# Local attention in blocks of 32 queries by 64 keys, with the queries' inverse norms applied inside the softmax

## The reference, cut to what matters

```
q, k, v = split(x @ Wqkv)                        # per layer; n = 1024, two sequences, 16 heads of 64
q = l2norm(q) * qs;  k = l2norm(k) * ksc         # t / max(norm(t), 1e-12)
q = q * cos * scale + rotate_half(q) * sin * scale
k = k * cos * inv   + rotate_half(k) * sin * inv
# windows of w = 32: a window's queries see its own keys and those of the window before
mask = (it < jb) | (it > jb + w) | (jb == -1)
sim  = where(mask, -max, einsum(q, k) * 8)
out  = einsum(softmax(sim), v) @ Wo
```

## Time and profile before

| | |
|---|---|
| median of 3 runs (lowest to highest) | 2109.58 us (2108.05 to 2110.93) |
| the profiled execution, its span | 2105.7 us, 2103.9 us |
| PE, DVE, ACT, POOL busy | 1906.2, 1582.6, 1596.2, 1665.0 us (91%, 75%, 76%, 79%) |
| mean granted TensorE clock | 0.973 of full speed |
| DMA queue of SP | 97.59 MB, 17.8% of 16 engines' span |

### The profile page before, as it was taken

One profiled execution on the slowest core, in us unless ns is written; L12 is line 12 of the kernel. 1 busy time (PEld: TensorE's weight loads), 2 busy tenths in 40 slices (PEclk: granted clock), 3 DMA queues, 4 the chain that ended last, 5 costly groups with the idle time before them and its releaser, 6 DMA issues.

```text
span 2103.9 us, 67397 instructions
## 1 busy us (share of the span) xinstructions
PE 1906.2 (91%) x22192; PEld 1444.0 (69%) x22192; DVE 1582.6 (75%) x4006; ACT 1596.2 (76%) x5607; POOL 1665.0 (79%) x1252
## 2 busy tenths in 40 slices
PE   5992899998999998899989899988999998999986
PEld 3661678774777774777774677774777774777772
DVE  4766788876788876788876788876788876888865
ACT  4871788885888884888874888884888875888872
POOL 2123999985999976899976899976899976999960
PEclk9995999999999999999999999999999999999998
DMA  2001222110321111211111311111211111112110
GB/s 64 14 12 51 79 50 56 45 46 11 99 51 45 45 46 31 83 48 45 45 46 28 84 50 45 45 46 35 81 46 45 45 46 36 47 45 56 49 29 21
DMA packets 44547, 99.43 MB, mean 47 GB/s; under 512 B 7344, under 2 KB 24208, under 8 KB 43504
## 3 DMA queue, kind: packets, MB, share of 16 engines
q1 hardware_dynamic: 44400, 97.59, 17.8%
HBM read 19.59 MB, written 1.05 MB: 10 GB/s over the span
## 4 chain that ended last, share of the span: by engine, by line
PE 70%; issue 12%; POOL 8%; ACT 5%; DVE 4%; POOLq 0%; DVEq 0%; DMA 0%; ACTq 0%; SPq 0%
PE bank L1124 9%; PE bank L1137 8%; PE bank L1151 7%; PE bank L1172 7%; PE bank L1117 7%; PE bank L1153 6%; PE bank L1158 6%; PE bank L1152 6%; PE bank L1108 3%; ACT kT L525 2%; POOL rn L321 2%; POOL ropeL L358 2%; POOL tsum L323 2%; PE bank L1164 2%; PE bank L1255 2%
## 5 line engine op out<-in xcount | busy, mean ns | idle before, releaser
L321 POOL TENSOR_TENSOR rn<-n2c,half_neg 128x8 f32<-128x8 f32 x384 | 636.4, 1657 | 81.8 <-DVE n2c L793 81.0
L487 ACT ACTIVATE prob<-bank,nmax 128x96 f32<-128x96 f32 x1536 | 501.2, 350 | 130.6 <-DVE nmax L743 130.4
L323 POOL TENSOR_TENSOR tsum<-tc_,ts_ 128x512 f32<-128x512 f32 x384 | 489.3, 1274 | 0.0
L326 POOL TENSOR_TENSOR w_nat<-tsum,rn 128x512 f32<-128x512 f32 x384 | 400.6, 1043 | 37.8 <-POOL tsum L323 15.1
L786 DVE TENSOR_REDUCE n<-nat 128x8 f32<-128x512 f32 x384 | 262.3, 683 | 138.2 <-ACT nat L503 126.8
L487 ACT ACTIVATION_READ_ACCUMULATOR prob<-bank,nmax 128x1 f32 x1536 | 331.4, 216 | 0.0
L743 DVE TENSOR_REDUCE nmax<-bank 128x4 f32<-128x384 f32 x384 | 196.1, 552 | 153.7 <-PE bank L1117 146.5
L496 ACT ACTIVATE pT<-bank 96x512 f32<-96x512 f32 x384 | 230.3, 600 | 74.6 <-PE bank L1124 72.4
L1151 PE MATMUL bank<-w_hi,xs 128*128 128x512 f32 x576 | 275.1, 478 | 12.6 <-DVE ts_ L796 9.7
L796 DVE TENSOR_TENSOR ts_<-bank,ropeL 128x256 f32<-128x256 f32 x768 | 285.8, 414 | 0.0
L1124 PE MATMUL bank<-idf,prob 128*96 128x128 f32 x1536 | 245.9, 284 | 42.9 <-ACT kT L525 28.2
(11 more groups left out here) (126 smaller groups left out, 3331.0 us busy)
## 6 DMA issues: line engine op xcount, KB each, us to landing
vspace<-v_nat SPq DMA_DIRECT2D x96, 384.0 KB, 4.0
vspace<-v_nat SPq DMA_DIRECT2D x96, 256.0 KB, 3.4
vspace<-v_nat SPq DMA_DIRECT2D x95, 128.0 KB, 2.3
nat<-w_qkv SPq DMA_DIRECT2D x5, 1536.0 KB, 8.0
wo<-w_o SPq DMA_DIRECT2D x6, 512.0 KB, 4.0
w<-w SPq DMA_DIRECT2D x6, 341.0 KB, 3.1
shared<-w_qkv SPq DMA_DIRECT2D x1, 1536.0 KB, 7.0
w<-w SPq DMA_DIRECT2D x6, 192.0 KB, 3.1
```

Of the source, the lines that this page charges most:

```text
L321: nc.gpsimd.tensor_tensor(rn[:, r, :], n2c[:, r, :], half_neg[:, 0:8], ALU.pow).then_inc(pool_step, 1)
L323: nc.gpsimd.tensor_tensor(tsum[:, r, :], tc_[:, r, :], ts_[:, r, :], ALU.add).then_inc(pool_step, 1)
L326: nc.gpsimd.tensor_tensor(w_nat[:, r, :].rearrange("p (h d) -> p h d", d=D), tsum[:, r, :].rearrange("p (h d) -> p h d", d=D), rn[:, r, :] ...
L487: last = nc.scalar.activation(prob[:, 4 * b + i, :], SB[b][:, i * SPAN:(i + 1) * SPAN], ACT.Exp, bias=nmax[:, p, 8 * G + 4 * b + i:8 * G + ...
```

## The change

The queries of a tile are taken in four blocks w of 32 (`BLOCKS`), each with the 64 keys that it can see (`SEEN`), instead of two halves of 64 with 96 keys. So the banks SB hold 4 x 64 columns rather than 4 x 96, the exponentials are 128x64, and two heads fill the 128 columns of one transpose. `transpose_probs` and `probs_out` run once per group rather than twice, and wait for all eight exponentials. `scores` and `weigh_values` issue 32 matmuls per group (64 instructions in a trace) rather than 16, each with 32 rather than 64 weight columns. The values lie in `vw` in four blocks and twice, by head parity, on partitions 0 to 63 and 64 to 127, moved by ten DMAs rather than three. `weigh_values` writes two banks (half of bank 5, part of bank 7).

The queries' inverse norms stay in `rnq`: POOL no longer multiplies the queries by them (two of four `L326` per tile go, and its loop now takes two tiles). `exps` gets them as a per-partition scale, and `maxima` writes the raw maximum into four spare columns of the score bank and multiplies it by `rnq` in a second instruction. `heads_out` multiplies in two instructions of 256 columns.

The order is rewritten too. On PE both halves of `project_out` stand together behind `transpose_heads(t, 3)`; ring bank 4 takes all transposed heads, bank 6 the probabilities and outputs. On ACT `square(t+1, 3)` stands ahead of `probs_out(t, 1)`. On DVE `residual` is for tile t-1, and stands between `rotary(t+1, 1)` and `maxima(t, 1)`.

```diff
@@ -17,0 +18,2 @@
+BLOCKS, SEEN = P // WIN, 2 * WIN
...
@@ -102 +106,2 @@
-        rn = sb("rn", [P, 2, 8])
+        rn = sb("rn", [P, 8])
+        rnq = sb("rnq", [P, 2, HEADS])
...
@@ -131 +137,3 @@
-        PJ, SB, OB, YB = bank[0:2], bank[2:4], bank[5], bank[7]
+        PJ, SB, YB = bank[0:2], bank[2:4], bank[7]
+        OB, O2 = bank[5], (bank[5][:, 0:HB // 2], bank[7][:, P:P + HB // 2])
...
@@ -247,2 +264,7 @@
-                eng.dma_start(vw[WIN:SPAN, p, 0, :], v_nat[0:HALF, p, :]).then_inc(v_seen[p], 16)
-                eng.dma_start(vw[:, p, 1, :], v_nat[WIN:P, p, :]).then_inc(v_seen[p], 16)
+                for b in range(2):
+                    eng.dma_start(vw[b * SEEN + WIN:(b + 1) * SEEN, p, 0, :].rearrange("p (g c) -> p g c", g=2),
+                                  four_heads(p, b, 0, WIN)).then_inc(v_seen[p], 16)
+                for w in range(1, BLOCKS):
+                    for b in range(2):
+                        eng.dma_start(vw[b * SEEN:(b + 1) * SEEN, p, w, :].rearrange("p (g c) -> p g c", g=2),
+                                      four_heads(p, b, (w - 1) * WIN, SEEN)).then_inc(v_seen[p], 16)
@@ -251 +273,7 @@
-                    eng.dma_start(vw[0:WIN, 1 - p, 0, :], v_nat[P - WIN:P, p, :]).then_inc(v_prev[1 - p], 16)
+                    for b in range(2):
+                        eng.dma_start(vw[b * SEEN:b * SEEN + WIN, 1 - p, 0, :].rearrange("p (g c) -> p g c", g=2),
+                                      four_heads(p, b, P - WIN, WIN)).then_inc(v_prev[1 - p], 16)
+            def four_heads(p, b, row, rows):
+                return v_nat[row:row + rows, p, :].rearrange("p (g b c) -> p g b c", g=2, b=2)[:, :, b, :]
...
@@ -321 +350,8 @@
-                    nc.gpsimd.tensor_tensor(rn[:, r, :], n2c[:, r, :], half_neg[:, 0:8], ALU.pow).then_inc(pool_step, 1)
+                    if r == 0:
+                        at_least(eng, p_ready, t * 4 - 4)
+                        nc.gpsimd.tensor_tensor(rnq[:, p, cols], n2c[:, r, :], half_neg[:, 0:8], ALU.pow).then_inc(pool_step, 1)
+                        eng.wait_ge(pj_dve, Q + 1)
+                        at_least(eng, tp_full, Q - 1)
+                        nc.gpsimd.tensor_tensor(w_nat[:, r, :], tc_[:, r, :], ts_[:, r, :], ALU.add).then_inc(w_ready, 1)
+                        continue
+                    nc.gpsimd.tensor_tensor(rn[:, :], n2c[:, r, :], half_neg[:, 0:8], ALU.pow).then_inc(pool_step, 1)
...
@@ -486 +523,2 @@
-                    head = 8 * G + 2 * i + b
+                    h = 2 * i + b
+                    slot = 2 * (h % 4) + h // 4
@@ -488,2 +526,4 @@
-                        prob[:, 4 * b + i, :], SB[b][:, i * SPAN:(i + 1) * SPAN], ACT.Exp,
-                        bias=nmax[:, p, 8 * G + 4 * b + i:8 * G + 4 * b + i + 1], accum_out=lsum[:, p, head:head + 1])
+                        probs[:, slot * SEEN:(slot + 1) * SEEN], SB[b][:, i * SEEN:(i + 1) * SEEN], ACT.Exp,
+                        scale=rnq[:, p, 8 * G + h:8 * G + h + 1],
+                        bias=nmax[:, p, 8 * G + 4 * b + i:8 * G + 4 * b + i + 1],
+                        accum_out=lsum[:, p, 8 * G + h:8 * G + h + 1])
@@ -492 +532 @@
-            def probs_out(t, G, b, at):
+            def probs_out(t, G, at):
@@ -494,3 +534,3 @@
-                eng.wait_ge(pt_full, t * 4 + (2 * G + b + 1))
-                at_least(eng, pv_done, t * 2 + G)
-                nc.scalar.activation(pT[:, 4 * b:4 * b + 4, :], RING[at][0:SPAN, :].rearrange("p (h q) -> p h q", h=4),
+                eng.wait_ge(pt_full, t * 2 + (G + 1))
+                at_least(eng, pv_done, t * 2 + (G - 1))
+                nc.scalar.activation(pT[:, 4 * G:4 * G + 4, :], RING[at][:, :].rearrange("p (h q) -> p h q", h=4),
...
@@ -599 +638,0 @@
-                    probs_out(t, 0, 0, 6)
@@ -602 +641 @@
-                    probs_out(t, 0, 1, 4)
+                    probs_out(t, 0, 6)
@@ -609,2 +648,3 @@
-                        heads_T(t + 1, 1 - p, 0, 6)
-                    probs_out(t, 1, 0, 4)
+                        heads_T(t + 1, 1 - p, 0, 4)
+                        square(t + 1, 3)
+                    probs_out(t, 1, 4 if closing else 6)
@@ -614 +653,0 @@
-                        square(t + 1, 3)
@@ -616,3 +655,2 @@
-                        heads_T(t + 1, 1 - p, 1, 6)
-                    probs_out(t, 1, 1, 6)
-                    heads_out_T(t, 0, 4)
+                        heads_T(t + 1, 1 - p, 1, 4)
+                    heads_out_T(t, 0, 4 if closing else 6)
...
@@ -743,3 +782,8 @@
-                    nc.vector.tensor_reduce(nmax[:, p, 8 * G + 4 * b:8 * G + 4 * b + 4],
-                                            SB[b][:, 0:4 * SPAN].rearrange("p (h k) -> p h k", h=4),
-                                            AX.X, ALU.max, negate=True).then_inc(max_ready, 1)
+                    nc.vector.tensor_reduce(SB[b][:, 4 * SEEN:4 * SEEN + 4],
+                                            SB[b][:, 0:4 * SEEN].rearrange("p (h k) -> p h k", h=4),
+                                            AX.X, ALU.max, negate=True).then_inc(raw_ready, 1)
+                for b in range(2):
+                    eng.wait_ge(raw_ready, t * 4 + (2 * G + b + 1))
+                    eng.wait_ge(pool_step, t * 6 + (1 + 3 * G))
+                    nc.vector.tensor_tensor(nmax[:, p, 8 * G + 4 * b:8 * G + 4 * b + 4], SB[b][:, 4 * SEEN:4 * SEEN + 4],
+                                            rnq[:, p, 8 * G + b:8 * G + 8:2], ALU.mult).then_inc(max_ready, 1)
@@ -750,2 +794 @@
-                hs = slice(8 * G, 8 * G + 8)
-                nc.vector.reciprocal(linv[:, p, hs], lsum[:, p, hs]).then_inc(linv_ready, 1)
+                nc.vector.reciprocal(linv[:, p, 8 * G:8 * G + 8], lsum[:, p, 8 * G:8 * G + 8]).then_inc(linv_ready, 1)
@@ -753,4 +796,7 @@
-                nc.vector.tensor_tensor(
-                    o_nat[:, G, :].rearrange("p (h d) -> p h d", d=D), OB[:, :].rearrange("p (h d) -> p h d", d=D),
-                    linv[:, p, hs].rearrange("p (h o) -> p h o", o=1).to_broadcast([P, 8, D]),
-                    ALU.mult).then_inc(o_evac, 1)
+                for b in range(2):
+                    h0 = 8 * G + 4 * b
+                    last = nc.vector.tensor_tensor(
+                        o_nat[:, G, b * HB // 2:(b + 1) * HB // 2].rearrange("p (h d) -> p h d", d=D),
+                        O2[b].rearrange("p (h d) -> p h d", d=D),
+                        linv[:, p, h0:h0 + 4].rearrange("p (h o) -> p h o", o=1).to_broadcast([P, 4, D]), ALU.mult)
+                last.then_inc(o_evac, 1)
@@ -918,2 +963,0 @@
-                        if not (isinstance(n, int) and n == 1):
-                            residual(t - 2, n - 2)
@@ -925,0 +970,2 @@
+                    if not opening:
+                        residual(t - 1, n - 1)
...
@@ -1108,2 +1153,2 @@
-                    nc.tensor.matmul(SB[b][:, 0:4 * SPAN], idb[:, :].bitcast(bf16),
-                                     msk[:, n, :].bitcast(bf16).rearrange("p (o k) -> p o k", o=1).to_broadcast([P, 4, SPAN]),
+                    nc.tensor.matmul(SB[b][:, 0:4 * SEEN], idb[:, :].bitcast(bf16),
+                                     mskB[:, n, :].bitcast(bf16).rearrange("p (o k) -> p o k", o=1).to_broadcast([P, 4, SEEN]),
@@ -1112,3 +1157,3 @@
-                    g, cols = 4 * G + i, slice(i * SPAN, (i + 1) * SPAN)
-                    for half in range(2):
-                        qs, ks = slice(half * HALF, (half + 1) * HALF), slice(half * HALF, half * HALF + SPAN)
+                    g, cols = 4 * G + i, slice(i * SEEN, (i + 1) * SEEN)
+                    for w in range(BLOCKS):
+                        qs, ks = slice(w * WIN, (w + 1) * WIN), slice(w * WIN, w * WIN + SEEN)
@@ -1121,2 +1166,3 @@
-            def transpose_probs(t, G, b, at):
-                eng.wait_ge(p_ready, t * 4 + (2 * G + b + 1))
+            def transpose_probs(t, G, at):
+                eng.wait_ge(p_ready, t * 4 + (2 * G + 2))
@@ -1124 +1170,2 @@
-                    last = nc.tensor.transpose(RING[at][0:SPAN, i * P:(i + 1) * P], prob[:, 4 * b + i, :], idf[:, :])
+                    last = nc.tensor.transpose(RING[at][:, i * P:(i + 1) * P], probs[:, 2 * i * SEEN:2 * (i + 1) * SEEN],
+                                               idf[:, :])
...
@@ -1130,2 +1177,7 @@
-                eng.wait_ge(v_seen[p], seen(t, p))
-                at_least(eng, v_prev[p], prev_in(t, p))
+                if G == 0:
+                    at_least(eng, y_free, t)
+                eng.wait_ge(v_seen[p], seen_block(t, p))
+                at_least(eng, v_prev[p], prev_block(t, p))
+                eng.sem_inc(pv_begun, 1)
@@ -1133,6 +1185,6 @@
-                    for b in range(2):
-                        head, a = 8 * G + 2 * i + b, (2 * i + b) * D
-                        for half in range(2):
-                            qs = slice(half * HALF, (half + 1) * HALF)
-                            last = nc.tensor.matmul(OB[qs, a:a + D], pT[:, 4 * b + i, qs],
```

(30 more changed lines are left out.)

86 lines of the change are left out of this document (46 added, 40 removed).

## The result

The changed kernel takes 2283.02 us (median of four runs, 2280.7 to 2284.46) against 2109.69: a ratio of 1.082, 95% interval 1.080 to 1.084. It is 173 us slower; 2280 was predicted. The profiled execution has a span of 2280.5 us, 176.6 more than before.

A forecast was written before the change was run, and what follows sets the result against it. POOL was taken to set the rate, PE close behind. 2105.7 + 135 (cycle over four engines) + 41 (clock) - 6 (POOL at layers' starts) = 2275.7 profiled; with 3.9 to the median, 2280 us, range 2085 to 2390.

The forecast's parts named there:

- the ring: Closed cycle of waits over four engines, the least a tile can take: 17.7 us against 16.2, +135 us.
- The exponentials: On ACT: second pointer +0.09 us, fewer columns -0.027, net +0.063 each, 0.381 apart, +1.0 us a tile for sixteen.
- The maxima: On DVE: first exponential starts 0.91 us behind the maxima in place of 0.59, bounds 0.59 and 1.2.
- Leg 1: From maxima(·, 0) to maxima(·, 1): 8.6 us, against 7.75 before.
- Leg 2: From maxima(t, 1) to the next maxima(·, 0): 8.9 us, against 8.71 in the tile shown.
- PE: Scores and values some 0.6 us each per group; own work falls from some 15.3 to 13; idle about 2.5 a tile.
- rival 4: The array doesn't take eight pieces, 26 ns an instruction: +2.2 us a tile, about 2475 us; chance 0.05.
- The clock: PE's clock falls behind its wait in one tile in three, 1.36 us each: 0.45 a tile, +41 us.
- The DMAs: Ten issues rather than three at 0.60 us, 6 us of SP a tile, hidden within 11 us.
- (1): Rival: PE's clock falls in every tile, 17.7 + 1.36 us, 2360 us; chance 0.20.
- (2): Rival: the exponentials' second pointer is hidden, cycle 16.3 us, clock holds, 2113 us; chance 0.10.
- (3): Rival: POOL's relief decides, cycle at 15.3 us, about 2020 us; chance 0.13.

The follow-up runs named there:

- Run 12: Kernel before, with the sum tc + ts of j = 3 done by DVE in place of POOL: 2110.0 us, ratio 0.9999.
- run 1: Kernel before, with each exponential taking its scale from a column of ones in place of the default immediate: 2209.0 us, ratio 1.047.
- run 4: Kernel after, with a constant as the exponentials' scale in place of the queries' inverse norms: 2135.9 us, ratio 1.011.
- run 7: Kernel after, with project_out's halves moved apart on PE and DVE's residual put behind maxima(t, 1): 2199.1 us, ratio 1.041.
- Run 6: Kernel after, with 14 matmuls whose result nobody reads in PE's wait ahead of transpose_probs(t, 1): 2243.9 us, ratio 1.063.
- run 10: Kernel after without the norms' half, with product 4 ahead of transpose_probs(t, 1), project_out and residual moved, and the sum of j = 3 on DVE: 2048.3 us, ratio 0.972.
- run 9: Kernel after, with product 4 ahead of transpose_probs(t, 1), project_out's halves moved apart and residual behind maxima(t, 1): 2138.7 us, ratio 1.013.

## Why the prediction was right, point by point

**What bounded the kernel before.** Here the prediction was wrong, without harm to its number: it said that POOL sets the rate, with PE close behind. Run 12 takes (1665.0 - 1581.6) / 96 = 0.87 us of POOL out of each tile, and the tile stays at 16.34. By the chain it was PE's own order of instructions that set the rate, though no run takes work off PE alone. I had passed over this line of the page of the kernel before; within a layer, from 669 to 702 us, PE's instructions make up 92% of the chain:

```profile
PE 70%; issue 12%; POOL 8%; ACT 5%; DVE 4%; POOLq 0%; DVEq 0%; DMA 0%; ACTq 0%; SPq 0%
```

With the pointer added (run 1) ACT has 36% of the chain and PE 27%: the ring holds. So it stood close below PE before: 1.16 of 1.49 us came through, and my estimate from this is a ring 0.3 us shorter than the tile. Three bounds lay within a few tenths of a microsecond, PE's order, the ring and POOL's 15.9. The number came out because the ring of the kernel after, at 17.55, is longer than all of them, whichever was the bound before.

**The exponentials.** Right: 0.381 forecast, 0.382 measured (3.06 / 8). The two terms by themselves: the pointer +0.09 (0.093 in run 1, and 0.093 between run 4 and after), the columns -0.027 (0.318 before, 0.291 in run 4). This was the step that decided, and it was read from two rows of other activations and the gap between an exponential and its accumulator read the earlier trace rows.

**The maxima.** The first exponential was forecast 0.91 behind them; 0.94 and 0.85 measured.

**Leg 1,** 8.6 forecast, 637.85 - 629.52 = 8.33 measured. `rotary` 1 starts at 6.13 (6.21 forecast). The residual was sized at 0.35 behind the rotary; its pieces overlap with the ends around them, and from 637.58 to 637.85 it is 0.27, as run 7 confirms with 0.26.

**Leg 2,** 8.9 forecast, 9.3 measured (in brackets the forecast): 4.20 to `transpose_probs` (4.2); 1.44 to the square (1.53); 1.45 to the copy of kT (1.44); 628.31 - 627.35 = 0.96 from there to the mask (0.65); 1.21 to the maxima (1.06). The two last terms were too small: I gave a copy 0.59 and a semaphore 0.06, but the mask started 0.34 behind the end of the copy; and the scores took longer, below. The errors of the legs cancel, and that is luck: 17.5 forecast without the loop's turn, 17.55 measured with it. The turn itself, 0.2 a tile in the sum, is hardly there after: intervals with and without it are 17.60 and 17.53.

**PE.** 64 scores take 637.73 - 636.94 = 0.79 us and 64 values 0.84 (from 629.75 in the tile before to the next product), where I took 0.6 for each. Eight pieces give 12 to 13 ns an instruction, half of before's 26; but twice as many instructions at half the price cost the same. PE's wait was 2.12, not 2.5: leg 1 was 0.27 shorter and `weigh_values(t, 0)` ended 0.2 later in the cycle.

The Trainium skill, "TensorE: Matmul & The Clock Gate", section "Wait — 56ns, not 53.3ns?", puts a floor of about 25 ns under the distance of two starts. These 12 ns lie under it: on separate pieces of the array, at 64 columns, the measurement decides against the rule, and rival 4 with it. The trace of the kernel before could have told so: its mean of 26 ns hides single starts, and three in four of the starts of its scores are 6 to 7 ns behind the last one.

**The clock.** 0.45 us a tile forecast as one in three at 1.36; measured 0.60 as 45 in 72 at 0.96. Both factors were off, in opposite ways. In the tile shown the clock held for 1.3 us behind the wait before it fell (the first stretch below, behind the wait, has 0.72 granted; the second, ahead of it, 1.00):

```profile
642.05:645.20 3.15, 3.15 (x15) 2.64 (x16) 1.50 (x4) 2.50 (x5) 1.94 (x2) 0.72 0.00 0
632.30:635.40 3.10, 3.10 (x26) 2.65 (x25) 2.02 (x5) 3.10 (x12) 1.13 (x1) 1.00 0.67 165
```

So not all of the stretch that I had priced was at the low level, which made the price smaller, and the fall behind waits of 2.1 us was more frequent than I took it. Run 6 gives 39 us back, beside the 41 of the sum.

**The DMAs.** Ten issues of 0.66 in place of 0.60 each. A tile's issues, below, are over by 634.2, five us ahead of `weigh_values` at 639.07. In the profile no instruction of the six layers waits for them, as said.

```profile
627.59 1.25 SPq L265 DMA_DIRECT2D vspace<-v_nat  x2
628.88 3.96 SPq L269 DMA_DIRECT2D vspace<-v_nat  x6
632.89 1.31 SPq L274 DMA_DIRECT2D vspace<-v_nat  x2
```

**The sum.** +135 (ring), +41 (clock), -6 (POOL at the layers' starts) forecast, 170 together. Measured: 1.34 and 0.60 a tile inside the layers, 166 us over all 90 intervals, and 11 us more outside them, 176.6 together. The gain at the layers' starts didn't come; what the 11 us are, no run shows. The ring was sized 0.15 a tile too long and the clock as much too short. The last 3.9 us of the forecast, from the profiled execution to the median, were 0.7 here. So the mechanism was right, but that 2280 lies within 3 us of 2283 is luck: each of its terms is off by more.

**The rivals.** (1) The clock in every tile: no, two in three. (2) The pointer hidden: runs 1 and 4 rule it out. (3) POOL's relief decides: run 12 rules it out for the kernel before, and in the kernel after POOL is idle for 4.7 us of a tile; the relief pays only once PE and the ring are shorter than POOL (run 10). Its 15.3 was also added up wrongly: 17.7 less 1.44 for the pointers, 0.64 for the maxima and 1 for the overlap is 14.6. (4) Ruled out by 12 ns an instruction.

## What to carry to other kernels

When every engine has idle time and each one's is ended by another, add up the links from start to start. What lies on the ring counts in full, down to one operand of one instruction, and what lies off it counts for nothing, even on an engine that is busy for 96% of the time, as POOL was. When two bounds are close, read the chain before the busy shares, and test which of them holds by taking work off one, before you pay on another engine for its relief. And look at what PE has queued behind its longest wait: moving instructions that all stay the same took 144 us off this kernel (run 9; 39 of them are the clock's, by run 6), while POOL's sum, moved off a bound, took 27 (run 10).
